# Moving three query-rotation multiplies on VectorE to the front of each step of a two-layer transformer kernel

## The reference, cut to what matters

```python
q = _rmsnorm(q, q_norm_w)
k = _rmsnorm(k, k_norm_w)
pos = cache_seqlens[:, None] + jnp.arange(seqlen)[None, :]
q = _rope(q, pos)          # [t1*cos - t2*sin, t2*cos + t1*sin]
k = _rope(k, pos)
...
scores = jnp.einsum('bqhd,bkhd->bhqk', q, k_all) * SCALE
scores = jnp.where(valid[:, None, None, :], scores, -1e+30)
probs = jax.nn.softmax(scores, axis=-1)
o = jnp.einsum('bhqk,bkhd->bqhd', probs, v_all)
```

## Time and profile before

| | us |
|---|---|
| median of 3 runs (2039.14 to 2040.28) | 2039.4 |
| the profiled execution, its own time | 2048.39 |
| its span | 2046.6 |

### The profile page before, as it was taken

How to read it: one execution, slowest core, us unless ns; L and a number is a source line. 1 busy time by engine, 2 the same in 40 slices (tenths; PEclk the granted TensorE clock), 3 DMA queues, 4 the chain that set the end, 5 groups by cost and what they waited for, 6 DMA issues and landing times.

```text
span 2046.6 us, 35827 instructions
## 1 busy us (share of the span) xinstructions
PE 1990.2 (97%) x12449; PEld 1696.5 (83%) x12456; DVE 1533.6 (75%) x3383; ACT 1323.5 (65%) x3796; POOL 801.8 (39%) x797
## 2 busy tenths in 40 slices
PE   6999999999999999999999999999999999999986
PEld 5778677888888888888888888888888888888873
DVE  6777764556666555687887888878878888888997
ACT  4676763545554554566776777767767777677785
POOL 3200015100000000056666666666666666666662
PEclk9999999999999999999999999999999999999998
DMA  7301101101201110121111111211111111112000
GB/s 259 98 28 48 53 1 73 62 32 37 68 32 51 43 53 1 58 78 32 62 53 31 62 51 31 82 32 53 61 32 62 53 32 63 53 32 83 26 28 36
DMA packets 45010, 108.60 MB, mean 53 GB/s; under 512 B 15634, under 2 KB 21010, under 8 KB 40354
## 3 DMA queue, kind: packets, MB, share of 16 engines
q1 hardware_dynamic: 28450, 72.74, 10.3%
q0 software_dynamic: 16384, 33.59, 5.6%
HBM read 103.14 MB, written 3.15 MB: 52 GB/s over the span
## 4 chain that ended last, share of the span: by engine, by line
PE 90%; DVE 5%; ACT 3%; issue 1%; DMA 1%; SPq 0%; DVEq 0%; ACTq 0%
PE PS L1662 10%; PE PS L1487 9%; PE PS L1430 9%; PE PS L1674 8%; PE PS L1566 8%; PE PS L1629 7%; PE PS L1647 7%; PE PS L1580 4%; PE PS L1443 4%; PE PS L1632 3%; PE PS L342 3%; PE PS L1458 3%; PE PS L1473 2%; PE PS L498 1%; PE PS L1465 1%; PE PS L1589 1%
## 5 line engine op out<-in xcount | busy, mean ns | idle before, releaser
L2517 POOL DMA_INDIRECT kcache<-in_kcache,rows x256 | 249.9, 976 | 533.4 <-DVE x_res L1818 462.4
L2525 POOL DMA_INDIRECT vcache<-in_vcache,rows x256 | 257.2, 1005 | 124.2 <-issue 58.4
L1991 DVE CUSTOM_DVE_ANT_0 pr<-PS,ffn_weights,sm 128x640 f32<-128x640 f32 x256 | 224.6, 885 | 88.6 <-PE PS L1632 88.6
L2007 DVE TENSOR_TENSOR prT_lo<-PS,prT_hi 128x512 fp32r<-128x512 f32 x320 | 209.2, 685 | 46.1 <-ACT prT_hi L2387 41.8
L2376 ACT ACTIVATE pr<-pr,sm 128x640 f32<-128x640 f32 x256 | 212.3, 831 | 40.1 <-DVE sm L1991 40.0
L2387 ACT ACTIVATE prT_hi<-PS 128x512 fp32r<-128x512 f32 x320 | 178.9, 597 | 78.5 <-PE PS L1647 67.3
L1647 PE MATMUL PS<-consts,pr 128*128 128x128 f32 x1280 | 174.0, 273 | 2.7 <-DVE prT_lo L2007 1.6
L1647 PEld LDWEIGHTS PS<-consts,pr 128*128 128x128 f32 x1280 | 149.7, 141 | 28.8 <-issue 3.7
L2531 POOL TENSOR_TENSOR vcached_lo<-vcache,vcached_hi 128x512 fp32r<-128x512 f32 x64 | 83.2, 1300 | 228.8 <-ACT vcached_hi L2359 228.6
L1629 PE MATMUL PS<-kT_hi,qT_hi 128*128 128x320 f32 x512 | 154.5, 310 | 2.2 <-DVE sm L1991 1.3
L1629 PE MATMUL PS<-kT_lo,qT_hi 128*128 128x320 f32 x512 | 154.1, 309 | 0.0
(11 more groups left out here) (319 smaller groups left out, 6173.3 us busy)
## 6 DMA issues: line engine op xcount, KB each, us to landing
arena<-in_wqkv SPq DMA_DIRECT2D x16, 1536.0 KB, 6.3
arena<-in_wo SPq DMA_DIRECT2D x16, 1024.0 KB, 5.4
arena<-in_wcT SPq DMA_DIRECT2D x8, 1024.0 KB, 6.6
kcache<-in_kcache,rows POOLq DMA_INDIRECT x256
vcache<-in_vcache,rows POOLq DMA_INDIRECT x256
arena<-in_xT SPq DMA_DIRECT2D x8, 256.0 KB, 8.2
x_res<-in_x SPq DMA_DIRECT2D x1, 2048.0 KB, 13.4
ffn_weights<-in_alibi SPq DMA_DIRECT2D x2, 1024.0 KB, 6.9
```

Source lines behind the costliest of these rows:

```text
L1991: dve.tensor_tensor_reduce(pr2[:, h, :].rearrange("p (a n) -> p a n", a=2), PS[:, SCORE_BANK[h]:SCORE_BANK[h] + 2, 0:HALF], keymask[:, b, ...
L2007: dve.tensor_tensor(prT2[1][:, n % 3, :, :].rearrange("p h n -> p (h n)"), bank(4 + n % 2), prT2[0][:, n % 3, :, :].rearrange("p h n -> p ...
L2517: pool.indirect_dma_start(out=kcache[:, c, :], out_offset=None, in_=T["kcache"], in_offset=bass.IndirectOffsetOnAxis(ap=rows[:, g, b, c:c ...
L2525: pool.indirect_dma_start(out=vcache[:, c, :], out_offset=None, in_=T["vcache"], in_offset=bass.IndirectOffsetOnAxis(ap=rows[:, g, b, c:c ...
```

## The change

In VectorE's step, `spread_q(i + 1)` goes to the very front, ahead of `hidden_steps` and the four `row_max`; `join_q(i + 1)` stays where `rotate_q(i + 1)` was. Nothing else is altered: no operation is added or removed, and the helper `rotate_q` goes.

```diff
@@ -1944,10 +1944,6 @@
                 dve.wait_ge(a2_rq, n + 1)
                 dve.tensor_tensor(qk2[:, 0:GH * P], qk2[:, 0:GH * P], swapped2[:, 0:GH * P], ALU.add).then_inc(a2_qr, 1)
 
-            def rotate_q(n):
-                spread_q(n)
-                join_q(n)
-
             def rotate_k(n):
                 g, b = group_of(n)
                 dve.wait_ge(a2_voh, n + 1)
@@ -2026,6 +2022,8 @@
                 more = i + 1 < ITEMS
                 new_weights, new_out = b == B - 2 and g < G - 1, b == 0
                 q = i - LAST
+                if more:
+                    spread_q(i + 1)
                 if q >= 4:
                     hidden_steps(q - 4, 1)
                 if q >= 2:
@@ -2039,7 +2037,7 @@
                 normalise(i, 1)
                 reciprocals(i, (2, 3))
                 if more:
-                    rotate_q(i + 1)
+                    join_q(i + 1)
                     rotate_k(i + 1)
                 if i + ITEMS - FROM_X < B:
                     lo_of_x(i + ITEMS - FROM_X)
```

## The result

| | before | changed |
|---|---|---|
| median of the runs, us | 2040.08 (6 runs, 2039.14 to 2040.95) | 2058.51 (6 runs, 2057.32 to 2062.37) |
| the profiled execution, us | 2048.39 | 2057.32 |
| its span, us | 2046.6 | 2054.8 |

The ratio is 1.0091, 95% interval 1.0081 to 1.0101: 18.4 us slower.

The account below looks back on a forecast made before the run. TensorE, busy 97% of the span, was taken as the bound, fed by VectorE's queue without slack. Delays of 6.6 + 10.6 + 0.8 + 7.9 = 25.9 us on 2039.4 gave 2065 us, range 2056 to 2073.

Parts of the forecast that it names:

- A row maximum that starts later by d therefore holds TensorE back by d.: VectorE's gapless run from first maximum to `lo_of_o`: any delay d of that maximum reaches TensorE in full.
- 8 x 0.83 = 6.6: Eight steps with b = 1: output-weight subtractions make the first maximum 0.83 us late, 6.6 us in total.
- The delay d = 1.51 with b = 6: Seven steps with b = 6: ScalarE's late squares hold up the multiplies, first maximum 1.51 us late, total 10.6.
- 0.07: Ordinary steps, 36 of them: multiplies end before the maximum can start, with 0.07 us to spare, so no delay.
- 0.11: Seven steps with b = 7: the first maximum starts 0.11 us later, total 0.8 us.
- The price of such a step is 0.83: Steps with b = 6 before the change: the first copy of transposed probabilities starts late, costing 0.83 us, mean over seven.
- The last items: Items 58 to 62, multiplies ahead of `hidden_steps`: first maxima late by 1.26, 0.85, 1.82, 1.96 and 1.96, sum 7.9 us.
- rival 4: Delays partly taken up, such as half of those in items 58 to 62: sum 22, about 2060 us, chance 0.08.
- Rival 1: Steps with b = 6: the shift cures the late copy of transposed probabilities; sum 22.2, 2061.6 us, chance 0.15.
- Rival 2: Steps with b = 1: the late copy appears there as well; sum 32.5, 2072 us, chance 0.15.
- Rivals 3 and 5: 3: ordinary steps late too, 3 to 5 us, chance 0.08; 5: TensorE follows VectorE's middle, ordinary steps shorten, chance 0.03.

Follow-up runs that it names:

- extra1: Changed kernel with one redundant repeat of the full-width cosine multiply in the 36 ordinary steps; 2060.69 us, ratio 1.0092 to the kernel before.
- extra2: Changed kernel with two redundant repeats of the full-width cosine multiply in the 36 ordinary steps; 2084.62 us, ratio 1.0213 to the kernel before.
- third profile of before: The kernel before, unchanged, run once more for its profile on the chip where before takes 2047.35 us; 2048.95 us, ratio 1.0007.
- before_again: The kernel before, unchanged, profiled a second time; 2044.83 us, ratio 1.0001.
- after_third: The changed kernel, unaltered, run and profiled a third time; 2058.55 us, ratio 1.0075 to the kernel before.
- weights_only: Kernel before with the multiplies in front only in the steps with b = 1, 6, 7 before item 58; 2054.89 us, ratio 1.0050.
- after_again: The changed kernel, unaltered, run and profiled a second time; 2059.48 us, ratio 1.0090 to the kernel before.
- behind_hidden: Changed kernel with the multiplies behind `hidden_steps`, directly ahead of the maxima, in the last items; 2057.89 us, ratio 1.0079 to the kernel before.
- ordinary_only: Kernel before with the multiplies in front only in the 36 steps before item 58 whose b is not 1, 6 or 7; 2043.91 us, ratio 0.9994.

## Why the prediction was right, and where its sum was off

**Direction and mechanism held.** The cost sits where it was put: at b = 1, at b = 6 and among the last items, nothing in the ordinary steps; it goes by the row maximum and `lo_of_o` to TensorE, and VectorE's saving in the middle becomes idle time. What did not hold is the size: the price of a late maximum (point 1), the delay with b = 6 (point 2) and the last items (point 4) were put too large, and one reading of before was wrong (point 3).

**1. "A row maximum that starts later by d therefore holds TensorE back by d."** This step failed. It took the 0.05 us between `lo_of_o` and the output projection as the whole slack, and "without a gap" as "as fast as it can". But the earlier trace rows show four maxima in 3.45 us, and they start 0.88 apart (1429.39, 1430.27, 1431.15, 1432.03): each was waiting for its score head. Late maxima find their heads ready and start 0.80 apart, which gives 0.24 back. `extra1` (17.17 us with 0.24 of lateness) and `extra2` (all of the next 0.72 paid) show it. It takes 0.24 from each of 22 steps, 5.3 us: 8 x 0.83 = 6.6 becomes 4.6 with b = 1.

**2. The delay d = 1.51 with b = 6.** ScalarE's squares were read from one execution, and there they were late themselves. The tail of an ordinary step in the third profile of before (the last matmul of `project_q`, then the first square; timeline of PE and ACT into item 32):

```profile
1441.88 0.39 PE L1566 MATMUL PS<-w_qkv_hi,xT_lo 128*128 128x512 f32 x1
...
1442.69 0.28 ACT L2344 ACTIVATE square<-PS 128x128 bf16<-128x128 f32 x1 [0.43 <-PE PS L1566]
```

and in the changed kernel:

```profile
1444.79 0.39 PE L1566 MATMUL PS<-w_qkv_hi,xT_lo 128*128 128x512 f32 x1
...
1445.22 0.28 ACT L2342 ACTIVATE square<-PS 128x128 bf16<-128x128 f32 x1
```

From the matmul's end to the square it is 0.42 us in the one and 0.04 in the other. The profile that the prediction used was of the first kind: its last square ends 1.37 us before the maximum, and in the changed kernel 1.79 before. It is not the change that brings this: in `before_again`, the kernel before with few late completions, it is 1.79 as well. Hence an ordinary step has 0.49 us to spare in place of 0.07 (1448.16 - 1447.75 + 0.08), and with b = 6 the delay is 18.29 - 17.17 = 1.12. With the maxima's 0.24 off, that step leaves 0.24 to the next, whose own delay then is 17.32 - 17.17 + 0.24 = 0.39, not 0.11. The two predicted delays, 1.62 together, were 1.51; their cost was 1.04.

**3. "The price of such a step is 0.83"**, the late first copy with b = 6. I treated it as a property of the order. In the third profile of before (timeline of PE and ACT, items 30 and 31), the transposes of the probabilities and the copy that waits for them:

```profile
1417.25 1.03 PE L1647 MATMUL PS<-consts,pr 128*128 128x128 f32 x8
...
1418.78 1.09 ACT L2387 ACTIVATE prT_hi<-PS 128x512 fp32r<-128x512 f32 x2 [1.10 <-PE PS L1647]
...
1435.18 1.03 PE L1647 MATMUL PS<-consts,pr 128*128 128x128 f32 x8
...
1435.93 1.09 ACT L2387 ACTIVATE prT_hi<-PS 128x512 fp32r<-128x512 f32 x2 [0.44 <-PE PS L1647]
```

With b = 6 the copy starts 1.53 us behind the transposes' start, with b = 7 0.75. How late goes with the chip, or with the moment, since each chip was used only once. Over the groups the step from b = 6 to b = 7 took 17.96 us where before ran at 2047.35, and 17.41 to 17.52 in three profiles where it ran at 2044.55; three of its seven steps in `before_again` took 17.17. I take it as 17.17 where before ran at 2041.23 and four other profiles showed no late completion (no profile of before exists there). Seven steps of 0.79 or some 0.3 are 5.5 or some 2 us; added to 2041.23 they give 2046.7 and 2043, near the two. The changed kernel took 2058.51, 2059.48 and 2058.55 beside a before of 2040.08, 2041.23 and 2043.79: it hardly feels the lateness (in `after_third` 17.40 against 17.32 in the mean into b = 7, and 22.40 against 22.07 into item 61). That fits the lower ratio of 1.0075 on the last, but no profile of before exists there, and the intervals of the three ratios overlap. The runs of before by which this case is timed were by their times of the undisturbed kind (2039 to 2041); its profiled execution (2048.39, 226 late completions) was not.

**4. The last items.** Predicted 7.9, measured 4.1 between item 57's and item 63's first maximum (124.76 against 120.66 in `before_again`), or 4.3 with the 0.24 that item 57 hands on. The single steps grew by 1.14 into item 58 (19.53 against 18.39 in `weights_only`, which has the same step 57), then 0.84, 1.17, 1.11 and 0.98 where 1.26, 0.85, 1.82, 1.96 and 1.96 stood; and 0.90 came back in the last step, which has no multiplies in front (20.16 against 21.06). The delays themselves were right: in items 60 to 62 the last square ends 3.25 us before the first maximum, in `before_again` 1.34, 1.28 and 1.33, so d is 1.91, 1.97 and 1.92. What failed is again the step of point 1, that TensorE is held back by all of d. The maxima give back some 0.2 in items 59, 61 and 62 (in 58 and 60 they ran 0.80 apart before the change too). And TensorE had other waits here that the late maxima cover: from item 57's to item 63's first maximum the idle time of its weight loads until a row maximum grew from 0.6 us in `before_again` to 6.6 in the changed kernel (both profiles), and that until `lo_of_o` from 0.5 to 1.6. But the idle time before the quantised feed-forward (L1745) fell from 4.3 to 3.4, before the transposes of the probabilities (L1647) from 3.4 to 1.9, and before `weigh` (L1662) from 1.8 to 1.5. So of 7.1 us of new waits some 2.7 replaced old ones, which leaves 4.4, near the 4.1 of the step lengths. That is the mechanism of rival 4.

The sum by step lengths: 4.6 + 7 x 1.04 + 4.3 = **16.2 us**, in place of 25.9. The two comparisons beside a before of 2040 to 2041 gave 18.4 (16.5 to 20.6) and 18.3 (15.1 to 21.4), the third, with perhaps 2 us of disturbance in before, 15. The 2 us that are missing are not placed. The profiles cannot place them: what lies outside the 63 steps took 939.0 to 943.6 us from one profile to the next, and 939.6 and 942.1 in `after_again` and `behind_hidden`, which ran on one chip and do not differ there.

**The rivals.** Rival 1, the copy with b = 6 on time, is what the changed kernel shows: its copy starts 7.49 us behind the first maximum (1413.91 to 1421.40), not 8.68. But it was not shown that the shift cured it: the changed kernel's steps into b = 7 are within 0.1 us of these in the mean with and without late completions, and where before was not disturbed (17.17 in three steps of `before_again`) it pays nothing for it either. Rival 2 did not come: with b = 1 the copy starts at 7.49 as well (1466.16 to 1473.65). Rival 4 holds for the last items: half of 7.9 was taken up, as it said, and the measured time lies nearest to its 2060. It did not have the catch-up of the maxima with b = 1 and b = 6. Rivals 3 and 5 fell with `ordinary_only`.

**Gather and normalisations.** Timeline of POOL and DVE in the changed kernel, first item 30 (b = 6), then item 33 (b = 1):

```profile
1417.78 0.95 POOL L2523 DMA_INDIRECT vcache<-in_vcache,rows  x1 [0.30 <-issue]
...
1417.91 1.14 DVE L1998 TENSOR_SCALAR pr<-pr,sm 128x640 f32<-128x640 f32 x2
...
1469.76 1.08 POOL L2523 DMA_INDIRECT vcache<-in_vcache,rows  x1 [0.30 <-issue]
...
1470.16 1.02 DVE L1998 TENSOR_SCALAR pr<-pr,sm 128x640 f32<-128x640 f32 x2
```

Both gathers began before the normalisations. The pair took 1.14 us with b = 6 and 1.02, its undisturbed length, with b = 1, so the lengthening by 0.15 that I built rival 2 on does not follow from the overlap alone. The Trainium skill (SBUF — State Buffer, the section on its two sides) has the first of the two hold the port pair for its whole instruction; by this VectorE would have stood until 1470.84 with b = 1. The trace does not agree there: it started at 1470.16 and took no longer. Nor does it in the earlier trace rows, where the prediction read agreement: the normalisations started at 1415.63, inside a gather of 1415.53 to 1416.48, and took 0.15 longer, not the 0.85 until its end. And where the lengthening did occur in the changed kernel, the copy was on time.

## What to carry to other kernels

When a queue feeds the busiest engine, ask of each of its operations whether it is as fast as it can be or is paced by the engine that it feeds: the difference between the two spacings (here 0.88 against 0.80, three times between four maxima) is slack that a gapless timeline does not show. Beyond it lateness is paid in full where the fed engine is never idle, and only in part where it has other waits (the last items here). Read delays that hang on a hand-over from an execution whose own time is near the median of the runs; when the two are 9 us apart, look for the hand-overs that stretched, before a late step is taken for a property of the order. Work in front of a wait-bound queue costs what sticks out behind its spare time, and placing it behind whatever need not wait for the same producer (`hidden_steps` here) saves the wait.

## What the runs showed of the hardware that was not expected

TensorE's completions can reach the other engines 0.1 to 1.4 us behind the modelled end of the matmul, and how many do differs between executions of the same program: the changed kernel had none in two profiles and some in the third. Counted as above, from 0.06 to 1.5 us late, there are 226 in the profile of before, 209, 201 and 199 on the chip where before takes 2047.35 us, 40 to 62 where it takes 2044.55, 44 where it takes 2043.79, and none where it takes 2041.23 (1989 semaphore updates each). These counts are too high, because a rise that the trace lacks is matched with the next one, which at the transposes of the probabilities comes 0.45 us later. Without such cases 166, 153, 139 and 140, 26 to 42, 28 and none are left. The missing rises go with the late ones: 157 to 302 in each profile with late completions, 0 to 14 in the others.

What is left gathers at the transposes of the probabilities, the output projection (0.5 in the median) and the query projection (0.4). The hand-over is late in fact and not only by the count: the first copy of transposed probabilities starts 8.65 to 8.68 us behind the first maximum with b = 6 in the first and third profiles of before, 8.01 in the mean in `before_again`, and 7.49 to 7.50 in all three of the changed kernel. In ordinary steps the lateness cost nothing: those took 17.17 us on every chip. Each chip was used at one moment only, so chip and moment cannot be told apart. Whether the completion is late or the matmul itself is slower than its modelled record, and why it costs time with b = 6 alone, stays open.
